# Moving 80 PSUM evictions from VectorE to ScalarE and changing a planner's hand-over cost, in an attention and FFN layer

## The reference

```
x = L0_attn_x                                     # (4, 4096, 1024) fp32
x = _layernorm(x + attn(x))                       # 16 heads of 64, causal softmax
x = _layernorm(x + ffn(x))
def act_quant_fake(x):
    scale = 127.0 / jnp.clip(jnp.max(jnp.abs(x), axis=-1, keepdims=True), EPS, None)
    return jnp.clip(jnp.round(x * scale), -128.0, 127.0) / scale
def weight_quant_fake(w):
    scale = 1.0 / jnp.clip(jnp.mean(jnp.abs(w)), EPS, None)
    return jnp.clip(jnp.round(w * scale), -1.0, 1.0) / scale
def ffn(x):
    h = layernorm(x, ln1_w, ln1_b)
    h = bitlinear(h, w1, b1)                      # 1024 -> 4096, both operands quantised
    h = jax.nn.gelu(h, approximate=False)
    h = layernorm(h, ln2_w, ln2_b)
    return bitlinear(h, w2, b2)                   # 4096 -> 1024
```

## Time and profile before

| | |
|---|---|
| time, median of 3 runs | 2729.02 us (2719.64 to 2763.33) |
| the profiled execution's own time | 2704.51 us |
| span of its slowest core (core 3) | 2703.0 us |
| the other cores | 2657.1 to 2695.1 us |
| busy, share of the span | PE 66%, ACT 51%, DVE 35%, POOL 9% |
| granted TensorE clock, core 3, mean | 0.798 of full speed |

### The profile page before, as it was taken

How to read it: one execution, slowest core, us unless ns; L and a number is a source line. 1 busy time by engine, 2 the same in 40 slices (tenths; PEclk the granted TensorE clock), 3 DMA queues, 4 the chain that set the end, 5 groups by cost and what they waited for, 6 DMA issues and landing times.

```text
span 2703.0 us, 31560 instructions; the slowest of 8 cores (2657.1 to 2703.0 us)
## 1 busy us (share of the span) xinstructions
PE 1778.2 (66%) x9412; PEld 686.6 (25%) x9412; DVE 951.5 (35%) x2196; ACT 1385.0 (51%) x2603; POOL 254.6 (9%) x454
## 2 busy tenths in 40 slices
PE   2999948788757777677674222177557675765766
PEld 1444422222221122222221112123222232222222
DVE  0111100000221112211325675355656555565644
ACT  0322217888559886377161222564545546454553
POOL 1000010000000000000000001203112131211303
PEclk9987879999876778888756555589788888887888
DMA  9111050000064310100103436405334252433415
GB/s 141 23 25 32 1 94 1 1 1 1 16 194 153 121 63 9 39 1 1 47 1 97 137 125 206 105 26 170 102 101 136 75 186 74 139 101 109 147 65 170
DMA packets 63004, 218.69 MB, mean 81 GB/s; under 512 B 12660, under 2 KB 12660, under 8 KB 60533
## 3 DMA queue, kind: packets, MB, share of 16 engines
q0 software_dynamic: 43040, 132.68, 18.3%
q1 hardware_dynamic: 16918, 67.21, 7.2%
q10 hardware_dynamic: 2880, 16.78, 1.8%
HBM read 227.64 MB, written 14.68 MB: 90 GB/s over the span
## 4 chain that ended last, share of the span: by engine, by line
PE 42%; ACT 17%; issue 16%; DVE 15%; DMA 8%; DVEq 1%; POOL 0%; ACTq 0%; SPq 0%; POOLq 0%
PE ps L464 9%; PE ps L1278 9%; ACT ptb L608 6%; PE ps L627 4%; PE ps L586 4%; ACT ptb L605 3%; PE ps L639 3%; PE ps L677 3%; PE ps L1530 3%; PE ps L563 2%; DVE cvx L1426 2%; DMA onesfb<-onesf 2%; DMA w2spill<-wstage 2%; PE ps L1282 1%; PE pt L950 1%
## 5 line engine op out<-in xcount | busy, mean ns | idle before, releaser
L605 ACT ACTIVATE ptb<-ps 128x512 bf16<-128x512 f32 (+7 forms) x640 | 337.6, 527 | 130.9 <-PE ps L643 90.8
L608 ACT ACTIVATE ptb<-ps 128x512 bf16<-128x512 f32 (+7 forms) x640 | 335.4, 524 | 0.0
L586 PE MATMUL ps<-QT,kvx 64*128 64x512 bf16 (+7 forms) x640 | 246.2, 385 | 129.3 <-ACT ptb L608 119.5
L1530 PE MATMUL ps<-kvx,q2t 128*128 128x512 bf16 x768 | 221.0, 423 | 85.0 <-DMA kvx<-w2spill 39.9
L627 PE MATMUL ps<-ptb,onescb 128*64 128x512 bf16 (+7 forms) x640 | 259.8, 406 | 19.8 <-DVE ptb L619 9.6
L639 PE MATMUL ps<-ptb,kvx 128*64 128x512 bf16 (+7 forms) x640 | 253.9, 397 | 28.1 <-DVE attnT L663 28.1
L1278 PE MATMUL ps<-kvx,q1t 128*128 128x512 bf16 x1024 | 261.1, 401 | 12.5 <-DVE q1t L1265 9.8
L631 PE MATMUL ps<-ptb,onescb 128*64 128x512 bf16 (+7 forms) x640 | 265.7, 415 | 0.0
L464 PE MATMUL ps<-xT,qkvw_sb 128*128 128x512 bf16 x1024 | 261.3, 414 | 5.9 <-DVE xT L454 5.9
L643 PE MATMUL ps<-ptb,kvx 128*64 128x512 bf16 (+7 forms) x640 | 255.0, 398 | 0.0
L616 DVE TENSOR_TENSOR ptb<-ptb,dmaskb 128x64 bf16<-128x64 bf16 x256 | 49.2, 192 | 580.4 <-ACT ptb L608 578.4
(11 more groups left out here) (166 smaller groups left out, 2753.4 us busy)
## 6 DMA issues: line engine op xcount, KB each, us to landing
kvx<-w2spill POOLq DMA_DIRECT2D x256, 256.0 KB, 4.3
wsbuf<-w2spill POOLq DMA_DIRECT2D x128, 256.0 KB, 3.8
wstA<-w SPq DMA_DIRECT2D x32, 512.0 KB, 4.8
wstA<-w SPq DMA_DIRECT2D x8, 2048.0 KB, 8.6
xkvbf<-xkv POOLq DMA_DIRECT2D x8, 1024.0 KB, 9.8
xres<-xq SPq DMA_DIRECT2D x16, 512.0 KB, 3.3
wbuf<-w ACTq DMA_DIRECT2D x16, 512.0 KB, 3.3
wbuf<-w SPq DMA_DIRECT2D x16, 512.0 KB, 3.5
```

The lines of the kernel that those rows point to most:

```text
L586: eng.matmul(ps[sA][:, noff:512], kt_ap(kb, p, 0, 64), QT[0:64, p * 512 + noff:(p + 1) * 512], start=True, stop=True, tile_position=(0, 0))
L605: eng.activation(ptb[:, ptA + noff: ptA + 512], ps[sA][:, noff:512], AF.Exp, bias=cSH, scale=c0125)
L608: return eng.activation(ptb[:, ptB + noff: ptB + 512], ps[sB][:, noff:512], AF.Exp, bias=cSH, scale=c0125)
L1530: r = eng.matmul(ps[4 + nn][:, 0:512], q2t[:, gb * 1024 + k * 128: gb * 1024 + (k + 1) * 128], rhs_ap(nn * 512, (nn + 1) * 512), start=(cc ...
```

## The change

Two things change. The copies of transposed activations out of PSUM, one into `q1t` and four into `q2t` per tile, 80 in all, are issued on ACT as an Identity activation instead of on DVE as a copy, and the planner is told 0.75 us for them. And the planner's hand-over cost `LAT` is 0.4 instead of 0.3, for the whole program.

```
-        LAT = 0.3
+        LAT = 0.4
...
         def feq1(eng):
-            return eng.tensor_copy(q1t[:, pq: pq + E], pt[gbq][:, 0:1024])
-        sd.step("vector", feq1, reads=[f"pt{gbq}", QN], writes=[QN],
-                name=f"f{ti}eq", dur=0.6)
+            return eng.activation(q1t[:, pq: pq + E], pt[gbq][:, 0:1024],
+                                  AF.Identity, bias=f32(0.0), scale=f32(1.0))
+        sd.step("scalar", feq1, reads=[f"pt{gbq}", QN], writes=[QN],
+                name=f"f{ti}eq", dur=0.75)
...
             def feq2(eng, gb=gb, pb=pb):
-                return eng.tensor_copy(q2t[:, gb * 1024:(gb + 1) * 1024],
-                                       pt[pb][:, 0:1024])
-            sd.step("vector", feq2, reads=[f"pt{pb}", f"q2t{gb}"],
-                    writes=[f"q2t{gb}"], name=f"f{ti}e2_{g}", dur=0.6)
+                return eng.activation(q2t[:, gb * 1024:(gb + 1) * 1024],
+                                      pt[pb][:, 0:1024], AF.Identity,
+                                      bias=f32(0.0), scale=f32(1.0))
+            sd.step("scalar", feq2, reads=[f"pt{pb}", f"q2t{gb}"],
+                    writes=[f"q2t{gb}"], name=f"f{ti}e2_{g}", dur=0.75)
```

## The result

The changed kernel ran in 2778.3 us (median of 8 runs, 2742.6 to 2797.9); the kernel before, again on the same chip, in 2713.3 (10 runs). The ratio is 1.018, 95% interval 1.012 to 1.025; it is not the quotient of these two medians, since ratios here compare only executions in which no half of the chip ran slower, at a lower clock, than the other. On a second chip, beside other experiments, it was 1.016 (1.013 to 1.019). So the change costs 1.6 to 1.8%. The forecast, 2754 us or +0.9%, had the sign and about half the size, and 2778.3 lies inside its range of 2715 to 2790. On the first chip the interval reaches over 2%, on the second it does not.

What follows compares the result with a forecast made beforehand. No engine fills the span: DVE leads the weight loop, the FFN is a chain hopping between engines, attention is ACT-bound. Terms 9 + 0 + 12.6 + 2 + 2 = +25.6 us on 2729.0 gave 2754 us (+0.9%), range 2715 to 2790.

Steps and rivals of the forecast that it cites:

- Weight loop, +12.6 us: First weight loop (w1): 0.4 reorders it so ACT's eviction no longer lies under g; +0.45 us a turn, 28 turns.
- The rival that the order costs nothing: Weight loop: t waits for the transposes in either order, so no loss there; total 2742 us; chance 0.13.
- Odd front, half B, +2.8: FFN, even mm1 to odd mm1: q1t copy behind two quantise steps delays odd mm1; +2.8 us a pair.
- Half A, -1.5: FFN, odd mm1 to next even mm1: q2t copies leaving DVE shorten it; -1.5 us a pair, bounds -2.5 and +1.
- the 117 to 118 that were to show it: FFN stage: sign that tile pairs would take 117 to 118 us instead of 116.4.
- First pair and tail, 0: FFN's first pair and the last tile's closing chain: gains and losses together 0 us (-3 to +3).
- Stores 0, start of the stores +2: 24 stores of w2 blocks behind the weight loop: length unchanged, start about 2 us later (0 to 4).
- Attention +2: Attention: absolute sums of w1 placed closer together, some 15 wait 0.15 us for loads; +2 us (-1 to +8).
- DVE relieved: FFN rival: DVE is pacemaker throughout, so 80 copies save 48 us; total 2698, 1.1% faster; chance 0.10.
- ACT's queue as the bound, slower by 2.3%: FFN rival: copies wait for whole 1 us ACT steps, 5 us a pair; total 2793 us; chance 0.12.
- the even copy behind its neighbours: FFN, within the ACT rival: the even tile's copy also falls behind neighbouring ACT steps; 2.2 us a pair.
- its own other terms (20 + 4 + 5): ACT rival's additions outside the FFN pairs: weight loop at its upper 20, hand-over 4, loads 5 us.

Runs made afterwards that it cites:

- e4: Kernel before, copies on DVE, with the planner's number 0.4 in the weight stage alone and 0.3 elsewhere: ratio 1.006 (1.003 to 1.010).
- e8: Changed kernel with the q1t copy of odd tiles, from the third on, put ahead of two quantise steps in ACT's queue: ratio 1.017 (1.012 to 1.022).
- e9: Changed kernel with half the w2 stream from tile 1 on and two buffers for g in the weight stage: pair 119.4 us, weight stage 206.2 us.
- e7: Kernel before with only the 64 q2t copies moved to ACT, planner's number 0.3: ratio 1.000 (0.998 to 1.002).
- e6: Kernel before with only the 16 q1t copies moved to ACT, planner's number 0.3: ratio 1.013 (1.009 to 1.017).
- e12: Kernel before with 0.4 outside the weight stage, and there each PSUM bank evicted by one engine under its own name: 2654.9 us, ratio 0.986.
- e10: Kernel before with half the w2 stream alone, from tile 1 on: pair 116.1 us, FFN 839.8 us.

## Why the prediction was right, and where its terms were off

- *Weight loop, +12.6 us.* Right in place and mechanism, too small: the 28 turns cost +15.9, and the stage +20.8 with what follows them. The sum from t to the second eviction was 2.57 us; it measured 2.75. The term mis-sized is the first: I took 1.20 us from t to g, the row of t followed by a small copy, and it is 1.40. The rest is that I let half the turns gain 0.12 us from a DMA issue on ACT; t to t rose by 0.66 over the last 24 of these turns and by 0.57 over all 28, not 0.45. The rival that the order costs nothing is out (e4).
- *Odd front, half B, +2.8.* By its own mark right: even to odd mm1 went from 48.47 to 51.2 on most cores, +2.7, with q1e 1.1 late and the copy behind two steps. But the step that takes the pair's length from that mark failed. The gelu behind it hangs on ACT's row as much, and e8 took 1.1 us off the mark with no gain. That the term comes near the 2.6 us by which the gelu is late (56.8 to 59.4) is therefore partly luck.
- *Half A, -1.5.* This step failed: half A is 68.8 us against 68.4 before, +0.4. The even transposes came 0.7 us nearer to the odd gelu instead of 1.5, and behind them mm1 lost 1.4 us, to two more matmuls and, place by place, to waits for the stream or to PE's lower clock. I had looked at what DVE saves, and not at what PE's order puts between transposes and mm1, nor at its clock. A pair is +3.4, not +1.3, in the median; it passed the 117 to 118 that were to show it (120.4 by these marks, which give 117.0 for before). From tile 2's to tile 14's first mm1 the mean of six pairs is 120.2 against 117.5, +2.7.
- *First pair and tail, 0.* On core 3 the first pair, from tile 0's LN step to tile 2's first mm1, is 2.7 us shorter (114.0 before, 111.3), within the bound; the tail is 3.6 us longer in the median, of which 2 are within its noise. The stage as a whole: +17.8 against +9.
- *Stores 0, start of the stores +2.* Stores were a little shorter in most runs with 0.4 in the weight stage (97.6 to 98.9 against 99.5 to 102.5; but 99.5 in the first execution of the changed kernel, and e9 with its two buffers 100.8). The later start is within the 20.8: what lies between the 28 turns and the first wstage copy grew by 4.7 us, more than the upper bound of 4.
- *Attention +2.* Not settled: medians of 671.0 to 675.5 at 0.3 and 672.9 to 676.0 at 0.4.
- *DVE relieved.* Out. DVE lost 44 us of busy time (55 forecast), ACT gained 75 (82 forecast), and e7 shows that 64 copies off DVE gain nothing. The rule of the Trainium skill ("Perfetto Trace Analysis", Optimizing Scalar/DVE Operations) that offloading may pay once DVE is saturated is not contradicted: DVE is full in stretches alone.
- *ACT's queue as the bound, slower by 2.3%.* Nearer than its chance of 0.12 says. A pair lost 3.4 of its 5 us, and e6 and e8 show that the queue is part of its mechanism; its other place, the even copy behind its neighbours, was not it. Its price for the verdict was also misread: with its own other terms (20 + 4 + 5) the 54.6 us of two per cent are reached at 3.7 us a pair, not 4.5.

The sum, +25.6, came out as +42 (20.8 + 17.8 + 3.6 + 3.7 of attention, which is partly noise, less 3.6 of the stores). Set on the forecast's base of 2729.0 that is 2771, inside the range. The sizes were off in the same direction in both stages, and neither helped to hide the other.

## What to carry to other kernels

An instruction moved to an idle engine pays its place in that engine's queue, and that can be more than its duration: ask what stands ahead of it, what then stands behind it, and what the next consumer needs besides. Where two conditions are tied, easing one at the other's cost gives nothing, so a mark that moves (mm1 earlier) is no proof until the period moves too. A planner's one constant can be good in one stage and bad in another; compare by stage. And a chain that alternates engines over one bank stayed in both orders tried here; giving each engine a bank and a name of its own removed it.

## What the runs showed of the hardware

- A DVE instruction that follows t starts 1.20 us after it when it is a 128x128 copy (1502.72 to 1503.91 in e12) and 1.40 us after it when it is the f32 compare (1505.87 to 1507.27), whether or not it depends on t (e9).
- The matmuls behind the even transposes followed each other at 0.41 us at a granted clock of 0.55 (e9), and at 0.24 at 1.00 (e10); 2.57 against 0.73 us of waiting went just before, but a wait of 3.47 us in e10 left the clock at 1.00.
- Halving the w2 stream's bytes shortened a pair by 1 us in both kernels, though on core 3 of the changed kernel mm2 (L1532) waited 70.0 us for the stream in all: most of that waiting is slack.
